# Folded weights, values four heads at a time, and a new order of the round in an audio tower

## The reference, cut to what matters

```python
# x: (32, 40000) -> 250 frames of 100 samples for each of 32 batches, 8000 tokens of width 192
power = |rfft(frame * window)| ** 2
mfcc  = log(power @ mel_filters.T + 1e-6) @ dct.T        # 51 bins -> 40 -> 13
h     = mfcc @ w_proj + b_proj                           # 13 -> 192
# attention block on layernorm(h): 8 heads, dk 64, dv 24, relative positions
h1 = rmsnorm(x, norm1_w); q, k, v = h1 @ wq, h1 @ wk, h1 @ wv
qw = einsum('bihd,hdn->bihn', q, w_pos)                  # 32 values a head and row
scores = (q k + qw . basis(j - i) + u k + (v_param . w_pos) . basis(j - i)) / 8
out = softmax(scores) @ v;  x = out @ wo + bo + x
x = x + gelu(rmsnorm(x, norm2_w) @ w1 + b1) @ w2 + b2
# feed forward on layernorm(h): 16 experts pick their best 1000 tokens each,
y = scatter_add(topk_score * ((silu(xg @ Wg.T) * (xg @ Wu.T)) @ Wd.T))
y = y + (silu(x @ Ws_g.T) * (x @ Ws_u.T)) @ Ws_d.T       # shared expert, all tokens
```

## Time and profile before

| | |
|---|---|
| median of 3 runs | 2253.63 us (2253.34 to 2255.13) |
| the profiled execution | 2256.45 us |
| its span, first to last instruction | 2254.7 us |
| PE busy | 2069.0 us, 92% |
| DVE busy | 1365.8 us, 61% |
| ACT busy | 1103.7 us, 49% |
| POOL busy | 704.0 us, 31% |
| one round of the tower (rounds 5 to 31) | 36.0 us |
| the tower | to 1244.7 us |
| feed forward | from 1244.7 us |

### The profile page before, as it was taken

One profiled execution on the slowest core, in us unless ns is written; L12 is line 12 of the kernel. 1 busy time (PEld: TensorE's weight loads), 2 busy tenths in 40 slices (PEclk: granted clock), 3 DMA queues, 4 the chain that ended last, 5 costly groups with the idle time before them and its releaser, 6 DMA issues. The chain is left out here.

```text
span 2254.7 us, 46810 instructions
## 1 busy us (share of the span) xinstructions
PE 2069.0 (92%) x13522; PEld 1700.7 (75%) x13522; DVE 1365.8 (61%) x3632; ACT 1103.7 (49%) x2680; POOL 704.0 (31%) x587
## 2 busy tenths in 40 slices
PE   2999999999999999999996699989999999999997
PEld 1677777777777777777774577778888888888886
DVE  1577767677776767677673577744555554555531
ACT  2677777767777777777763222122222222222221
POOL 0122122121212212121221000236665566665563
PEclk9899999999999999999997899999999999999998
DMA  5555655555555655555561633325454444454442
GB/s 142 156 146 147 168 143 163 148 158 151 151 163 144 167 147 155 150 156 161 143 165 50 161 103 102 93 54 89 91 97 77 73 78 88 91 98 76 73 80 31
DMA packets 317544, 272.43 MB, mean 121 GB/s; under 512 B 80740, under 2 KB 304822, under 8 KB 317494
## 3 DMA queue, kind: packets, MB, share of 16 engines
q1 hardware_dynamic: 238374, 235.01, 39.0%
q0 software_dynamic: 70656, 30.65, 9.6%
q10 hardware_dynamic: 8464, 6.15, 0.9%
HBM read 150.73 MB, written 120.54 MB: 120 GB/s over the span
## 5 line engine op out<-in xcount | busy, mean ns | idle before, releaser
L1134 POOL DMA_INDIRECT out<-ff_y,ff_idxs x128 | 261.8, 2045 | 245.5 <-DVE ff_y L1417 187.9
L1194 ACT ACTIVATE ff_sg<-ffp_g 128x500 f32<-128x500 f32 x192 | 112.9, 588 | 400.3 <-PE ffp_g L1529 369.9
L1121 POOL DMA_INDIRECT ff_xg<-xs_d,ff_idxg x128 | 205.1, 1603 | 297.1 <-issue 283.6
L468 ACT ACTIVATE sb_prob<-sb_ssb,sb_mx 125x250 f32<-125x250 f32 x512 | 253.1, 501 | 58.6 <-DVE sb_mx L562 58.6
L1541 PE MATMUL ffp_d<-ff_wd,ff_wide 128*125 128x192 f32 x1536 | 261.2, 327 | 16.0 <-DVE ff_wide L1404 15.2
L1404 DVE TENSOR_TENSOR ff_wide<-ff_sg,ffp_u 128x500 f32<-128x500 f32 x192 | 129.4, 674 | 221.1 <-PE ffp_u L1529 219.5
L1541 PEld LDWEIGHTS ffp_d<-ff_wd,ff_wide 128*125 128x125 f32 x1536 | 247.8, 188 | 19.9 <-issue 18.2
L1529 PE MATMUL ffp_g<-ff_xsp,ff_wsp 128*128 128x500 f32 x960 | 251.8, 392 | 1.6 <-DVE ff_xsp L1276 1.6
L1529 PE MATMUL ffp_u<-ff_xsp,ff_wsp 128*128 128x500 f32 x960 | 249.6, 390 | 0.0
L548 DVE COPY sb_ptsb<-ps_ptps 125x500 f32<-125x500 f32 x256 | 172.9, 675 | 123.8 <-PE ps_ptps L716 120.6
L1529 PEld LDWEIGHTS ffp_g<-ff_xsp,ff_wsp 128*128 128x128 f32 x960 | 180.2, 189 | 39.3 <-issue 2.7
(11 more groups left out here) (181 smaller groups left out, 3664.4 us busy)
## 6 DMA issues: line engine op xcount, KB each, us to landing
bias_d<-sb_rsb SPq DMA_DIRECT2D x256, 219.6 KB
sb_bsk<-bias_d SPq DMA_DIRECT2D x256, 218.8 KB
hx_d<-sb_hx SPq DMA_DIRECT2D x32, 336.0 KB
sb_hxl<-hx_d SPq DMA_DIRECT2D x32, 336.0 KB
ff_wd<-WdT SPq DMA_DIRECT2D x16, 576.0 KB
xs_d<-sb_xs SPq DMA_DIRECT2D x32, 238.0 KB
bias_d<-sb_rsb SPq DMA_DIRECT2D x256, 25.5 KB
sb_bsk<-bias_d SPq DMA_DIRECT2D x256, 25.4 KB
```

The source lines that it names most:

```text
L468: a.activation(prob[:, s % 2, t], ssb[:, s % 2, t], ACT.Exp, bias=mx[:, s % 2, t:t + 1], scale=-1.0, accum_out=rs[:, t, s:s + 1]).then_inc ...
L1121: g.indirect_dma_start(xg[:, t], None, xs_d[:, :], bass.IndirectOffsetOnAxis(idxg[:, t:t + 1], 0), bounds_check=last).then_inc(gat, 16)
L1134: g.indirect_dma_start(out_d[:, :], bass.IndirectOffsetOnAxis(idxs[:, t:t + 1], 0), y[:, t], None, bounds_check=last, compute_op=ALU.add). ...
```

## The change

- The position weights are multiplied into wq once, at the start (16 small products, `folded`), and the result is split as further columns of `wsp`. `qw` comes straight from the normed input, two products of five parts a round in slots 1 and 5, each for four heads; `u_param` drops out of `cq`. Likewise dct and `w_proj` are multiplied once into `wmel`, and the mfcc stage is gone.
- `quad_values` replaces `pair_values`: four heads at once, twice a round, with four buffers `ptsb`.
- `row_inverses` uses transposes.
- The order in each round's slots is new on all engines: row copies (`pt_copy`) stand ahead of splits and statistics, the first product of q and k ahead of the values in slot 0, the `vtmp` copies are VectorE's, the residual add of GpSimd comes after the scaling, the router transposes go into slot 3 and `cps`, the third part of w1 into `tps`, the table load ahead of the exponentials.
- The shared expert's buffers live through both blocks. Its weights and first tokens are loaded in round 34 and split in round 35 of the tower, ahead of that round's other work on ScalarE and VectorE.

```diff
-        T_USES, C_USES, D_USES, Q_USES = 5, 5, 3, 18
...
+        T_USES, C_USES, D_USES, Q_USES = 4, 5, 3, 16
...
-        QK_USE = [0, 4, 10, 14]
-        QW_USE = [1, 5, 11, 15]
-        V_USE = [6, 7]
-        R_USE = [2, 3, 8, 9, 12, 13, 16, 17]
...
+        QK_USE = [0, 4, 9, 13]
+        QW_USE = [1, 10]
+        QW_SLOT = {1: 0, 5: 1}
+        V_USE = [5, 6]
+        R_USE = [2, 3, 7, 8, 11, 12, 14, 15]
...
+            def load_shared():
+                for i, src in enumerate((w["WsgT"], w["WsuT"])):
+                    sp.dma_start(sh.wraw[:, i, 0], src[0:128]).then_inc(sh.ld, 16)
+                    for half in range(2):
+                        sp.dma_start(sh.wraw[half * 64:half * 64 + 64, i, 1], src[128:D]).then_inc(sh.ld, 16)
+                for dst, src in ((sh.wd[:], w["WsdT"].rearrange("(k p) n -> p k n", p=128)), (sh.blocks[:], w["blocks"])):
+                    sp.dma_start(dst, src).then_inc(sh.ld, 16)
+                sp.wait_ge(c_st, 80 * (CHUNK // FRAMES))
+                sp.dma_start(sh.xraw[:, 0, 0], xnT_d[0:128, 0:CHUNK]).then_inc(sh.x_ld[0], 16)
+                for half in range(2):
+                    sp.dma_start(sh.xraw[half * 64:half * 64 + 64, 0, 1], xnT_d[128:D, 0:CHUNK]).then_inc(sh.x_ld[0], 16)
...
+                    if bc is not None and s == 4:
+                        apart(pool, READY, (c_ch, C_CHAIN * bc + C_CHAIN))
                         g.tensor_tensor(xb[:], x1[:], hxl[:, :, 0:D], ALU.add).then_inc(c_xb, 1)
...
+            def shared_high():
+                act.wait_ge(sh.ld, 16 * 8)
+                for i in range(2):
+                    a.activation(sh.wsp[:, i, 0], sh.wraw[:, i, 0], ACT.Copy).then_inc(sh.w_hi, 1)
+                    a.activation(sh.wsp[:, i, 2], sh.wraw[:, i, 1], ACT.Copy).then_inc(sh.w_hi, 1)
+                act.wait_ge(sh.x_ld[0], 48)
+                for k in range(2):
+                    a.activation(sh.xsp[:, 0, 0, k], sh.xraw[:, 0, k], ACT.Copy).then_inc(sh.x_hi, 1)
...
+                            v.tensor_copy(vtmp[:, t], qps[V_USE[t] % 2][0:TP, 0:D]).then_inc(q_ev[V_USE[t] % 2], 2)
...
+                    wait(dve, pv_mm, HEADS * b + h - h % QUAD)
+                    v.tensor_copy(ptsb[:, h % QUAD], ptps[:]).then_inc(pt_ev, 1)
...
+            def shared_low():
+                for i in range(2):
+                    for k, half in ((0, slice(0, 128)), (1, slice(64, 128))):
+                        dve.wait_ge(sh.w_hi, 2 * i + k + 1)
+                        v.tensor_tensor(sh.wsp[half, i, 1 + k], sh.wraw[half, i, k], sh.wsp[half, i, 2 * k].bitcast(F32), ALU.subtract).then_inc(sh.w_lo, 1)
+                for k in range(2):
+                    dve.wait_ge(sh.x_hi, k + 1)
+                    v.tensor_tensor(sh.xsp[:, 0, 1, k], sh.xraw[:, 0, k], sh.xsp[:, 0, 0, k].bitcast(F32), ALU.subtract).then_inc(sh.x_lo, 1)
...
+                if bc is None and bd is not None:
+                    shared_low()
...
+                    if bq is not None and s in QW_SLOT:
+                        use = QW_USE[QW_SLOT[s]]
+                        done = 4 * bq + 2 * QW_SLOT[s]
+                        halves = slice(0, 64), slice(64, 128)
+                        dve.wait_ge(q_mm, Q_USES * bq + use + 1)
+                        for i in range(2):
+                            p = 2 * QW_SLOT[s] + i
+                            v.tensor_scalar(qw[halves[i], i], qps[use % 2][halves[i], 0:FRAMES], cq[halves[i], p:p + 1], None, ALU.add).then_inc(qw_hi, 1)
+                        for i in range(2):
+                            p = 2 * QW_SLOT[s] + i
+                            dve.wait_ge(qw_hi, done + i + 1)
+                            v.scalar_tensor_tensor(out=qw[halves[1 - i], i], in0=qps[use % 2][halves[i], 0:FRAMES], scalar=cq[halves[i], p:p + 1],
+                                                   in1=qw[halves[i], i].bitcast(F32), op0=ALU.add, op1=ALU.subtract).then_inc(q_ev[use % 2], 1)
...
-            pe.wait_ge(ini, 1)
             for p in range(PAIRS):
-                ins = m(tps[:, p:p + 1], wpz[:, p].rearrange("d r i n -> d (r i n)"), vmu[:, p:p + 1], start=True, stop=True)
-            ins.then_inc(cq_mm, 1)
...
+                for k in range(2):
+                    for i in range(2):
+                        rows = slice(64 * i, 64 * i + 64)
+                        m(folded(i, k)[:, p], wqT[rows, p, k * 128:(k + 1) * 128], wpz[rows, p, 0, i], start=True, stop=True)
+            m(qps[1][0:MELS, 0:D], dct[:], wproj[:], start=True, stop=True)
+            for p in range(PAIRS):
+                ins = m(qps[0][:, p:p + 1], wpz[:, p].rearrange("d r i n -> d (r i n)"), vcol[:, p:p + 1], start=True, stop=True)
+            ins.then_inc(fold_mm, 1)
+            pe.wait_ge(ini, 9)
...
-                            ins = m(tps[:, k * FRAMES + t * TP:k * FRAMES + (t + 1) * TP], each, ident[0:TP, 0:TP], start=True, stop=True)
+                            ins = nc.tensor.transpose(tps[:, k * FRAMES + t * TP:k * FRAMES + (t + 1) * TP], each, ident[0:TP, 0:TP])
...
-            def pair_values(b, p):
+            def quad_values(b, k):
 
                 if b is not None:
-                    h = 2 * p
-                    if h % QUAD == 0:
-                        pe.wait_ge(vz_in, 2 * b + 1 + h // QUAD)
-                    if h == 0:
+                    pe.wait_ge(vz_in, 2 * b + 1 + k)
+                    if k == 0:
                         wait(pe, ot_ev, b)
-                    pe.wait_ge(pt_ev, HEADS * b + h + 2)
+                    pe.wait_ge(pt_ev, HEADS * b + QUAD * (k + 1))
                     for j in range(NT):
-                        for i in range(2):
-                            c = VC * ((h + i) % QUAD)
-                            ins = m(otps[c:c + VC, h // QUAD], vz[:, j, h + i], ptsb[:, i, j], start=j == 0, stop=j == NT - 1)
+                        for i in range(QUAD):
+                            ins = m(otps[VC * i:VC * i + VC, k], vz[:, j, QUAD * k + i], ptsb[:, i, j], start=j == 0, stop=j == NT - 1)
                             if j == NT - 1:
                                 ins.then_inc(pv_mm, 1)
 
+            def qk(b, p):
+
+                q_freed(pe, b, QK_USE[p])
+                if p == 0:
...
+                    if bq is not None and s in QW_SLOT:
+                        use = QW_USE[QW_SLOT[s]]
+                        q_freed(pe, bq, use)
+                        col = ALL_COLS + 128 * QW_SLOT[s]
+                        for k, (wk, xp, xk) in enumerate(PARTS):
+                            ins = m(qps[use % 2][:, 0:FRAMES], wsp[:, wk, col:col + 128], hsp[:, xp, xk], start=k == 0, stop=k == len(PARTS) - 1)
+                        ins.then_inc(q_mm, 1)
...
+                    if bq is not None and s == 0:
+                        qk(bq, 0)
+                    if s == 0:
+                        quad_values(bc, 1)
```

More of the change, by code:

```diff
@@ L332, in body @@
             def body(bt, bq, bb_, bc, bd):
+                if bb_ is None and bc is not None:
+                    load_shared()
                 for s in range(SLOTS):
@@ L497, in body @@
                         a.activation(gT[:, 1], ps[:, 1], ACT.Gelu, bias=b1[:, 1:2]).then_inc(c_ev, 1)
[L498 to L504, removed]
-                        act.wait_ge(t_mm, T_USES * bt + 4)
[L506 to L520, removed]
+                        act.wait_ge(c_mm, C_USES * bc + 4)
+                        a.activation(gT[:, 2], tps[:, 0:FRAMES], ACT.Gelu, bias=b1[:, 2:3]).then_inc(c_ev, 1)
+                    if bt is not None and s == 7:
+                        act.wait_ge(t_mm, T_USES * bt + 4)
                         if bq is not None:
@@ L860, in body @@
                             ins.then_inc(q_mm, 1)
+                    if bd is not None and s == 3:
+                        pe.wait_ge(c_sg, 2 * bd + 2)
+                        if bc is not None:
+                            pe.wait_ge(c_ev, C_USES * bc + 1)
+                        for t in range(NT):
+                            ins = nc.tensor.transpose(cps[0:EXPERTS, t * TP:(t + 1) * TP], xs[:, t, 256:SROW], ident[0:TP, 0:TP])
+                        ins.then_inc(d_mm, 1)
+                    if bt is not None and s == 4:
+                        pe.wait_ge(t_ev, T_USES * bt + 2)
+                        ps = bank2(tps, D, TP)
+                        for t in range(NT):
+                            ins = m(ps[:, t], logmel[:, t * TP:(t + 1) * TP], wmel[:], start=True, stop=True)
+                        ins.then_inc(t_mm, 1)
@@ new lines, in body @@
+                    if bc is not None and s == 4:
+                        if bd is not None:
+                            pe.wait_ge(d_ev, D_USES * bd + 3)
+                        pe.wait_ge(c_ch, C_CHAIN * bc + C_CHAIN)
+                        pe.wait_ge(c_ev, C_USES * bc + 1)
+                        transposes(bank2(cps, FRAMES, 128), h2n, c_mm)
+                    if bq is not None and s == 4:
+                        qk(bq, 2)
```

(11 more changed lines are left out.)

402 lines of the change are left out of this document (188 added, 214 removed).

## The result

The changed kernel takes 2096.05 us (median of four runs, 2095.07 to 2100.0), the kernel before 2253.49 beside it: ratio 0.9309, 95% interval 0.9288 to 0.933. The forecast was 2124 with a range from 2098, so the kernel is faster than the range allowed, by 2 us. The profiled execution's span went from 2254.7 to 2093.5, 161.2 less where the working had 129.9.

The account below looks back on a forecast made before the run. TensorE's queue was taken to bound the tower's middle. Full rounds -111.7, other rounds -14.2, start +4.6 and entry -8.6 sum to -129.9: 2256.45 becomes 2126.5, less 2.8 of excess over the median, 2124 us; range 2098 to 2182.

Parts of the forecast that it names:

- the subtractions ahead of the last drain: Round 35: six VectorE subtractions, 3.6 us, ahead of the last batch's normalization, 0.9 of it beside GpSimd's power; +2.7 us.
- entry proper: Feed-forward block's entry: first product 0.3 behind the barrier, second pair at +4.8 instead of +16.1; -11.3 us.
- the sum of a full round: Tower's middle: TensorE's group and wait savings of 4.89 leave 31.10, plus 0.9 of waits, 32.0 us instead of 35.99.
- waits, net: TensorE, per full round: today's four waits go, -1.41 us, and 0.9 of waiting is put back.
- A new wait on hsp at the turn of the round: Turn of the round: the first q/k product waits 0.3 us for VectorE's low half of hsp.
- The 0.2 ahead of the values: Turn of the round: values of the last four heads wait 0.2 us for VectorE's last row copy.
- The 0.25 for what the walk doesn't see: Full round: allowance of 0.25 us for TensorE waits not found going slot by slot, between 0 and 1.56.
- the floor of 31.10: Full round: 35.99 us less 4.89 of TensorE savings, before any new waits are added.
- VectorE's 0.7 for h2n: Full round: VectorE's first h2n scaling takes 0.31 instead of 1.05 us once GpSimd's residual add comes afterwards.
- Rival 1: Full rounds: values run only two wide, 2177 us, or TensorE waits 2.0 a round or more, 2157; chance 0.28.
- Rival 2: Full rounds: the bias's DMA round trip binds, the round stays at 36 us, 2250 in all; chance 0.04.
- Rival 3: Full rounds: more, if shorter, TensorE waits lower the granted clock; at a 30% share 2320 us; chance 0.08.

Follow-up runs that it names:

- e6: Changed kernel with the shared expert's loads, copies and subtractions back at the entry of the feed-forward block, behind the barrier: 2103.24 us, ratio 0.9337.
- e11: Changed kernel with VectorE's six shared-expert subtractions at the end of its rounds instead of ahead of the last normalization: 2095.87 us, ratio 0.9292.
- e1: Changed kernel with the values of four heads in the same places and buffers but issued two by two: 2094.67 us, ratio 0.9295.
- e5: Changed kernel with the row inverses again as products with the identity instead of transposes: 2109.94 us, ratio 0.9358.
- e2: Changed kernel with one wait added, the second v product waiting for VectorE's copy of the first: 2126.89 us, ratio 0.9443.
- e3: Changed kernel with the third w1 group back in the bank that the first group's gelu must leave, nothing placed between: 2183.2 us, ratio 0.9698.
- e10: Changed kernel with ScalarE's third gelu moved one slot on, behind the copy TensorE waited 0.28 for: 2097.55 us, ratio 0.9295.
- e8: Changed kernel with GpSimd's residual add again right behind its power, beside VectorE's scaling of h2n: 2099.76 us, ratio 0.9321.
- e4: Kernel before with only the values of four heads at once (four buffers, slots 0 and 4): 2289.01 us, ratio 1.0146.
- e9: Changed kernel with the low half of hsp ahead of the statistics in VectorE's queue of slot 7: 2143.36 us, ratio 0.9534.
- e7: Changed kernel with the two v copies on ScalarE again, at the place in slot 3 where VectorE has them: 2124.17 us, ratio 0.9424.

## Why the prediction was wrong in size and right in kind

The ledger, on the two profiled executions (forecast, then measured): start +4.6, +3.2; 28 full rounds -111.7, -130.0; the rounds at both ends, with the subtractions ahead of the last drain, -11.5, -20.4; entry proper -11.3, -10.7; the rest of the feed-forward block 0, -3.4. Sum -129.9, -161.3. The feed-forward block beyond its entry isn't edited; behind the second pair of products it takes 993.9 us before, 990.4 after, 989.3 in e6 and 992.3 in e11, so that -3.4 is within the scatter.

**The step that failed is the sum of a full round**: 32.0 forecast, 31.33 measured, 18 us over 28 rounds. Group by group, from start to start over one round of each trace (forecast, measured):

```
values          -1.78  -1.91     v products    0    -0.45
row inverses    -0.46  -0.63     scores        0    -0.35
qw              -0.72  -0.52     w1            0    -0.19
dct             -0.52  -0.52     all others    0    +0.32
waits, net      -0.51  -0.40
```

- The prices of edited groups were near: 3.48 forecast, 3.58 measured. Four heads at once run at the full factor (the windows after, and e1; the forecast had this from two, its reason why nothing should be lost was argued only), e5 gives the row inverses 0.48 where 0.46 was said, and the folded q products have their 0.69 and 0.67. The removed qw products were 0.52 each in the forecast, but 1.88 and not 2.08 together: the third takes 0.24 (615.93 to 616.17) before the v products start, and the rest is booked to them. Qw and v products as one fell by 0.97, where 0.72 was forecast. These prices are read from the two traces; no run undoes the folds or the four-wide values alone in the new order.
- The waits' net was near by luck. A new wait on hsp at the turn of the round was named and stands, but it is 0.73 and not 0.3. The 0.2 ahead of the values isn't there, and the 0.28 for a copy in slot 6 wasn't named. The 0.25 for what the walk doesn't see was a guess. And the sum counts 0.15 of today's idle twice, since the floor of 31.10 holds it already: 4 us over 28 rounds. In all 0.9 was added to the floor, and the waits are 1.01.
- What the sum lacked is that **waits were priced at their named idle, and groups which the edits don't touch at their old durations**. That cost three terms that the forecast put at nothing: v products 0.45, scores 0.35, w1 0.19. Of the 0.45, 0.28 is the booking above and 0.17 is left; e2 puts one such wait back and finds 0.21 in the groups, beside 0.81 named, and e3 shows the worse form, where the wait also costs the clock behind it. That a wait costs more than its idle is shown for these two. e10 shows the bound of the rule: a wait of 0.28 cut to 0.15 gave nothing. The 0.35 of the scores can be placed in the trace before, though no run tests it. The four groups took 1.11, 1.25, 1.11 and 1.05 without their named waits; the first three stand ahead of basis products that came late, and the 1.25 holds an idle of 0.14 (610.00 to 610.14) too short to be named. After, each takes 1.04. Why other groups, the transposes most, got longer by 0.32 stays open.
- **The ends**: I scaled full rounds down (3.0 and 1.5 for rounds 32 and 33), as these are "more and more bound by latency". They lost 5.5 and 5.1. With stages missing, the third w1 group waited 1.74 and 2.15 for the gelu there instead of 0.27, and at the second of these waits the clock fell to half for 3.4 us; its own bank takes that away. e3 puts 4.5 of the 11.8 us of rounds 32 to 35 on this one edit; the rest isn't split up by a run. These two rounds gained more from the removed waits than a full one, not less. The subtractions ahead of the last drain cost 3.8 in e11's trace where 2.7 was said.
- The start: the first spectrum product stands at 33.22 (34.6 forecast). The 32 instructions of the folds took 3.56 (3.7 said), the copies and subtractions 1.93 (2.5); another 0.8 was in the forecast's own 34.1, which its terms (24.8 + 6.0 + 2.5) don't give.
- The entry was right: 0.19 and 5.39 against 0.3 and 4.8, 7 to 8 us as a whole by e6 (8.6 said).
- VectorE's 0.7 for h2n was right (0.32 for the first scaling, 0.31 said) and worth nothing that shows (e8).
- **Rival 1** fell with the windows (two wide) and with an idle of 1.07 a round (waits of 2.0). **Rival 2**: no wait on a load, at 0.64 of the DMA engines. **Rival 3** didn't come about, with the clock at 1.00 in the round, but e4 and e3 show that it was real and near: the same value groups in the old order make the kernel slower. What spoke against it was "waits of up to 0.7 leave the clock at 1.00 today", and the changed kernel's longest is 0.73 as well; in e4, with 1.04, the clock fell. The stretch of the earlier trace rows that it calls round 34 begins 7 us before the end of round 33.
- By the Trainium skill's figure for four row tiles ("TensorE: Matmul & The Clock Gate", Part 3) a group would have taken 1.36, an estimate; it takes 0.98, so this trace shows no such loss for four column groups.

## What to carry to other kernels

In a kernel bound by one in-order engine, price a removed wait as idle plus what the groups on both sides were stretched by and what the clock lost behind it, and look for it also in the rounds where fewer stages run. It is an upper bound where another wait stands in the same round (e10). Parts of such a change don't add up: making the bound engine quicker in one slot takes cover from the others, so the quicker groups and the order that feeds them belong together (the values +36 us alone, the whole change -157). Before putting an instruction earlier in a queue, list what it now stands ahead of: e9 traded 0.5 for 1.7.

## What the runs showed of the hardware

- Four value products of 32 columns each run side by side at the full factor: sixteen instructions in 0.98 us, where a single product of the same 250 columns takes 0.52 for its two. Issued pair by pair they still do (e1, 0.99 and 1.01): TensorE starts a later product in free columns beside earlier ones that are still running.
- A transpose of a 125x128 float32 tile costs half of the product with the identity or less: four for 0.52 against eight instructions for 0.98 before, and in the changed order 0.35 against 0.82 (e5).
- With one wait of TensorE of 2.16 (e3), 1.04 (e4, beside one of 0.9 and shorter ones) or 1.73 (e9) in every round, the granted clock fell to 0.50, that is 1.2 GHz, for 3.4 us around or behind it, in 19, 23 and 9 of 26 middle rounds; a score group in such a stretch took 1.96 instead of 1.04 (e3). With longest waits of 0.73 (after), 0.81 (e2) and 0.85 (e7) it fell in none of them. So the length of the single wait alone doesn't decide: 1.73 brought the fall less often than 1.04.
